# Two mixture-of-experts layers around a causal linear attention: every expert on every token, or tokens grouped by expert through DRAM

## What is computed

```python
def _L0_ffn_ref(h, router_w, rn_g, rn_b, w1, ln_g, ln_b, w2, on_g, on_b):
    h_norm = layer_norm(h, rn_g, rn_b)
    g = jax.nn.softmax(jnp.einsum('bsd,ed->bse', h_norm, router_w), axis=-1)
    top2_w, top2_idx = jax.lax.top_k(g, 2)
    top2_w = top2_w / (jnp.sum(top2_w, axis=-1, keepdims=True) + EPS_GATE)
    hid = jnp.einsum('bsd,edh->bseh', h, w1)               # 4 experts, 256 -> 512
    hid = jax.nn.relu(layer_norm(hid, ln_g, ln_b))
    expert_out = jnp.einsum('bseh,ehd->bsed', hid, w2)     # 512 -> 256
    ...
    out = jnp.sum(top2_out * top2_w[..., None], axis=-2)   # the two best experts
    return layer_norm(out, on_g, on_b)
x = x + 0.5 * _L0_ffn_ref(_layernorm(x), ...)
x = x + _L0_attn_ref(_layernorm(x), ...)   # 16 heads of 16: V K^T summed over the tokens so far, times Q
x = x + 0.5 * _L0_ffn_ref(_layernorm(x), ...)
```

## Time and profile before

| | us |
|---|---|
| median of 3 runs | 1239.57 |
| lowest and highest run | 1239.57, 1240.85 |
| span of the profiled execution | 1236.4 |
| preparation, to the first matmul of layer 1 | 63.3 |
| first mixture layer (63.3 to 513.2) | 449.9 |
| attention (513.2 to 809.5) | 296.3 |
| second mixture layer (809.5 to 1225.7) | 416.2 |
| behind its last matmul | 10.7 |

### The profile page before, as it was taken

One profiled execution on the slowest core, in us unless ns is written; L12 is line 12 of the kernel. 1 busy time (PEld: TensorE's weight loads), 2 busy tenths in 40 slices (PEclk: granted clock), 3 DMA queues, 4 the chain that ended last, 5 costly groups with the idle time before them and its releaser, 6 DMA issues.

```text
span 1236.4 us, 25066 instructions
## 1 busy us (share of the span) xinstructions
PE 1140.2 (92%) x8694; PEld 731.9 (59%) x8694; DVE 948.3 (77%) x2150; ACT 512.8 (41%) x878; POOL 672.0 (54%) x1039
## 2 busy tenths in 40 slices
PE   4669799999999999889999999889999999999996
PEld 4335456656566566656666666556566665666664
DVE  5678787887978878657777777578879787797875
ACT  4353324233342424456665666442333424334131
POOL 2365546454565544498778777543555654546360
PEclk9789989999999999999999999899999999999998
DMA  9002000000000000000000000000000000000000
GB/s 286 4 1 69 1 1 2 1 2 1 0 0 0 1 2 1 19 18 15 11 13 18 17 18 18 1 2 2 17 1 18 1 19 18 0 17 1 19 18 17
DMA packets 29037, 20.69 MB, mean 17 GB/s; under 512 B 7812, under 2 KB 27784, under 8 KB 28808
## 3 DMA queue, kind: packets, MB, share of 16 engines
q1 hardware_dynamic: 24112, 18.36, 5.4%
q10 hardware_dynamic: 4824, 1.07, 0.5%
HBM read 11.03 MB, written 4.19 MB: 12 GB/s over the span
## 4 chain that ended last, share of the span: by engine, by line
PE 48%; DVE 19%; issue 16%; POOL 10%; ACT 4%; DMA 2%; DVEq 1%; ACTq 0%; POOLq 0%
PE bank L1547 7%; PE bank L1549 6%; PE bank L1548 6%; DVE area L674 5%; DVE area L682 4%; PE bank L1532 4%; PE bank L1534 4%; PE bank L1533 4%; DVE area L655 4%; PE bank L1506 4%; POOL area L487 3%; PE bank L1555 2%; PE bank L1557 2%; PE bank L1556 2%; DMA betas<-in_L_ffn_ln_b_dram 2%
## 5 line engine op out<-in xcount | busy, mean ns | idle before, releaser
L1256 ACT ACTIVATE area<-area 128x512 f16<-128x512 f32 x256 | 160.9, 630 | 387.9 <-DVE area L674 386.1
L1547 PE MATMUL bank<-w2h,area 128*128 128x256 f16 x1024 | 281.3, 275 | 12.9 <-DVE area L693 7.2
L1548 PE MATMUL bank<-w2l,area 128*128 128x256 f16 x1024 | 280.5, 274 | 0.0
L1549 PE MATMUL bank<-w2h,area 128*128 128x256 f16 x1024 | 280.5, 274 | 0.0
L674 DVE SCALAR_TENSOR_TENSOR area<-area,betas,bank 128x512 f32<-128x512 f32 x256 | 189.9, 743 | 46.0 <-PE bank L1534 37.6
L682 DVE SCALAR_TENSOR_TENSOR area<-area 128x512 f16<-128x512 f32 x256 | 188.7, 737 | 20.3 <-ACT area L1256 17.1
L1532 PE MATMUL bank<-hTh,w1h 128*128 128x512 f16 x512 | 195.5, 382 | 6.7 <-DVE area L674 6.7
L1533 PE MATMUL bank<-hTl,w1h 128*128 128x512 f16 x512 | 195.1, 381 | 0.0
L1534 PE MATMUL bank<-hTh,w1l 128*128 128x512 f16 x512 | 194.9, 381 | 0.0
L696 DVE SCALAR_TENSOR_TENSOR area<-bank,coef,area 128x256 f32<-128x256 f32 x192 | 92.1, 482 | 79.3 <-PE bank L1549 78.1
L487 POOL TENSOR_TENSOR area<-area 128x512 f16<-128x512 f32 x96 | 119.9, 1274 | 45.1 <-ACT area L1300 44.9
(11 more groups left out here) (233 smaller groups left out, 2109.6 us busy)
## 6 DMA issues: line engine op xcount, KB each, us to landing
X<-in_L_attn_x_dram SPq DMA_DIRECT2D x8, 512.0 KB, 7.1
area<-area SPq DMA_DIRECT2D x128, 32.0 KB, 2.0
out_dram<-X SPq DMA_DIRECT2D x7, 512.0 KB, 2.9
area<-in_L_ffn_w_dram SPq DMA_DIRECT2D x4, 512.0 KB, 9.9
X<-in_L_ffn_w_dram SPq DMA_DIRECT2D x2, 1024.0 KB, 15.7
area<-in_L_ffn_ln_g_dram ACTq DMA_DIRECT2D x1, 1024.0 KB, 6.1
out_dram<-X SPq DMA_DIRECT2D x4, 128.0 KB, 1.7
area<-in_L_attn_Wq_dram SPq DMA_DIRECT2D x1, 256.0 KB, 9.2
```

Source lines behind the costliest of these rows:

```text
L1256: act.activation(Rh[:, e % 2, m, :], V[:, a % NV], ACT.Relu).then_inc(s_Rh, 1)
L1547: pe.matmul(dst, Rh[:, e % 2, k, rows], w2h[:, e, k, :], start=(k == 0), stop=False)
L1548: pe.matmul(dst, Rh[:, e % 2, k, rows], w2l[:, e, k, :], start=False, stop=False)
L1549: last = pe.matmul(dst, Rl[:, e % 2, k, rows], w2h[:, e, k, :], start=False, stop=(k == HC - 1))
```

## The change

A mixture layer no longer runs every expert on every block. Its 32 tiles are two groups of 16. For each group:

- **Routing** goes by quads of four tiles. Row statistics (bn_stats and bn_aggr) are on DVE, the powers on POOL, the normalised rows on ACT as float16 high parts with DVE's low parts (`hrow`), the transposes, logits and a prefix sum of the choices (a triangular matrix) on PE, the softmax on ACT and DVE. DVE then gives each token and chosen expert a place in that expert's region (`place`), and at the end of a group tables: for each of 35 slot tiles of 128 places its expert (`etab`) and first row in DRAM (`rtab`), and for each token where its two results will lie (`pos`).
- **Scatter.** POOL writes each tile's rows (high and low part, 1 KB a token) to DRAM by indirect DMAs, one for the first and one for the second choice of the tile's tokens, 32 in a group, and four with rows of zeros behind the last token of each expert.
- **Slot tiles**, 35 in a group and 70 in a layer, run in 35 pairs. For each, SP reads its row number from the table into a register, loads the 128 rows plainly (`hs`, two pairs deep) and once more by a transposing DMA (`hT`, three pairs deep). PE reads the expert's number into a register and addresses all its weights by it: w1, w2 and the Gram matrices are now an array for each chunk, indexed by expert. The variance is computed for one expert, its root on POOL (`pair_std`), and PE transposes its two float16 parts to a row which DVE writes into partition 0 of `hT` (`std_rows`). Beta is row 0 of the chunk of w1 that meets it: one input row of w1 was subtracted from all others beforehand, as normalised rows have a zero sum. Layer 1 has thereby beta in its product; `hidden`, V, `sdB` and `sel` are gone, and ACT and DVE take the relu's parts from the bank. Layer 1 has 128 columns, layer 2 256 as before.
- **Results.** ACT scales a slot tile's result to SBUF (`scale_out`) and SP stores it to DRAM. For each token tile POOL gathers the first and the second expert's rows by two indirect DMAs, two tiles deep; ACT multiplies the first by its gate, DVE adds the second, normalises and adds to X. In the last layer SP stores each tile of X.

The next group is routed inside the pairs 0 to 13 of the layer (row statistics from pair 0, scatters in pairs 4 to 11, pads in 12), and the first group's tokens are gathered in pairs 19 to 28. The second group's 16 token tiles follow behind the last pair. The second layer's first group is routed ahead of its first pair. Attention is as before but stands alone: its weights' preparation and its first block do not lie in a mixture block, and no block of the second layer is prepared in its last chunks. All hardware loops are written out. The maxima over partitions in the preparation (POOL before) are transposes and small matmuls on PE.

```diff
+            def load_slots(S):                                   # SP
+                G, J = group(S)
+                if J == 0:
+                    for k in range(GQ):
+                        sp.wait_ge(sc_h[k], 32 * TB * (G + 1))
+                    sp.wait_ge(sc_p[G % 2], 16 * E * (G // 2 + 1))
+                    sp.wait_ge(r_tab, G + 1)
+                r, k = S // 2 % R_HS, S % 2
+                wait(sp, b_h2, S // 2 - R_HS + 1)
+                row = sp.value_load(rtab[0:1, G % 2, J:J + 1], min_val=0, max_val=(E - 1) * REG + (GT - 1) * P)
+                sp.dma_start(hs[:, r, k].rearrange("p c d -> p (c d)"),
+                             slots_in[G % 2][bass.ds(row, P), :]).then_inc(l_hs[S % (2 * R_HS)], 16)
+                wait(sp, b_A, 2 * (S // 2 - R_HT + 1))
+                sp.dma_start_transpose(hT[:, S // 2 % R_HT, k], slots_in[G % 2][bass.ds(row, P), :]
+                                       ).then_inc(l_hT[S % (2 * R_HT)], 16)
...
+                for k in range(2):                               # POOL, scatter(Q, j)
+                    pool.indirect_dma_start(slots_in[G % 2],
+                                            bass.IndirectOffsetOnAxis(spos[:, Q % 2, k, j:j + 1], 0),
+                                            hrow[:, t].rearrange("p c d -> p (c d)"), None
+                                            ).then_inc(sc_h[Q % GQ], 16)
...
+            def gather(i):                                       # POOL
...
+                wait(pool, c_acc, i - R_C + 1)
+                for k, d in enumerate((yA, yB)):
+                    pool.indirect_dma_start(d[:, i % R_C], None, slots_out[G % 2],
+                                            bass.IndirectOffsetOnAxis(pos[:, G % 2, k, t:t + 1], 0)
+                                            ).then_inc(g_y[i % R_C], 16)
...
+            def expert(S):                                       # PE
...
+                return pe.value_load(etab[0:1, G % 2, J:J + 1], min_val=0, max_val=E - 1)
...
             def layer1(...):
-                cols = slice(m * P, (m + 1) * P)
-                o = bank[m][:, :]
-                for c in range(KC):
-                    pe.matmul(o, w1h[:, e, c, cols], hTh[:, par, c, :], start=(c == 0), stop=False)
-                    pe.matmul(o, w1h[:, e, c, cols], hTl[:, par, c, :], start=False, stop=False)
-                    last = pe.matmul(o, w1l[:, e, c, cols], hTh[:, par, c, :], start=False, stop=(c == KC - 1))
+                a = hT[:, p % R_HT, S % 2]
+                for m in range(HC):
+                    o = bank[S % 2][:, m * P:(m + 1) * P]
+                    for c in range(KC):
+                        pe.matmul(o, w1h[c][m][:, bass.ds(e, 1), :], a[:, c], start=(c == 0), stop=False)
+                        pe.matmul(o, w1h[c][m][:, bass.ds(e, 1), :], a[:, KC + c], start=False, stop=False)
+                        last = pe.matmul(o, w1l[c][m][:, bass.ds(e, 1), :], a[:, c], start=False, stop=(c == KC - 1))
...
+                for p in range(NP):                              # PE, mixture(f)
+                    S = 2 * (p0 + p)
+                    if 1 <= p <= GP:
+                        rows_T(u1 + p - 1)
...
+                    if p + 1 < NP:
+                        nxt = [expert(S + 2), expert(S + 3)]
+                        grams(p0 + p + 1, nxt)
+                    layer1(S, e[0])
+                    if p >= 1:
+                        layer2(S - 1, last)
+                    layer1(S + 1, e[1])
+                    if 1 <= p <= GP:
+                        router(u1 + p - 1)
+                    if p + 1 < NP:
+                        std_T(p0 + p + 1)
+                    layer2(S, e[0])
+                    last, e = e[1], nxt
+                layer2(S + 1, last)
```

2165 lines of the change are left out of this document (1125 added, 1040 removed).

## The result

| | us, median | to the kernel before, with 95% interval |
|---|---|---|
| before | 1239.57 | |
| changed | 1433.46 (1426.42 to 1434.17) | 1.155 (1.152 to 1.158) |

A forecast was written before the change was run, and what follows sets the result against it. The prediction took the mixture layers to be bound by the PE array, DVE next. 70 pairs at 11.0 us, 770, plus 640 outside the pairs gave a span of 1410 and a time of about 1415 us, range 1190 to 1680.

The forecast's parts named there:

- The array's need is 357 us less: Mixture layers' matmuls on PE: 140 slot tiles at 3.08 us, 431 us, in place of 788.
- Light pairs at 10.5 us: PE's cost of two slot tiles with nothing beside them: matmuls, register steps, expert loads, transposes; 6.8 to 15.9.
- Pairs with tokens at 11: Nine later pairs of a layer, with two tokens summed and normalised on DVE beside them: 11 us each.
- The ring: Dependency through DVE, PE and ACT from one pair to the next: 11.7 us with a choose, 9.9 without.
- First matmul of layer 1 at 112: Preparation and first routing: 63 us before the change, together 112 after it.
- 64 us behind each layer: 16 tokens gathered, weighted and normalised with nothing beside them, POOL and DVE alternating at 3.5 us each.
- The second routing 75: Second layer's first group routed with nothing beside it: 18 us to positions, 36 scatters at 1.2, 12 to fill.
- All seams: 640 forecast: Everything outside the pairs: preparation 112, tokens behind layers 128, attention 320, second routing 75, last stores 5.
- The signs: What the changed kernel's profile should show if the forecast holds, such as PE well under 70% busy in mixture layers.
- A: Rival, chance 0.20: register steps and loads hide behind the array; pairs 8.6 to 9.9 us, span 1242 to 1333.
- C: Rival, chance 0.17: faster than before, PE remaining array-bound with less array time; 1107 to 1237 us.
- B: Rival, chance 0.19: dearer register steps, loads, register-addressed matmuls or transposing DMA; 13 to 15.5 us a pair, 1550 to 1725.

The follow-up runs named there:

- fixed_expert: Changed kernel with PE taking weights at fixed addresses, no expert number loaded (wrong experts): 1359.4 us.
- the other series: Later side-by-side measurement in which the unaltered changed kernel took 1399.8 us, where the first gave 1433.5.
- std_early: Changed kernel with DVE doing the next pair's std parts right behind its variances, ahead of token and routing steps: 1351.1 us.
- gather_deep: Changed kernel with buffers for gathered tokens four tiles deep and not two: 1423.3 us.
- plain_scatter: Changed kernel with plain DMAs to fixed rows from POOL for the indirect scatters and pads (results wrong): 1377.5 us.
- plain_T_again: Changed kernel with plain DMAs of the same bytes for the transposing ones (results wrong), repeated beside the unaltered changed kernel: 1398.8 us.
- changed_again: The changed kernel itself, unaltered, measured again in a later series: 1399.8 us.
- loads_only: Changed kernel with expert numbers loaded and checked but unused, all weights at fixed addresses (wrong experts): 1330.2 us.
- both: Changed kernel with std parts early on DVE and fixed experts without loads together (wrong experts): 1231.1 us, 0.994 of the kernel before.
- one_load: Changed kernel with one expert number loaded per mixture layer and used for all its slot tiles (wrong experts): 1357.9 us.

## Why the prediction was right, point by point

Slower was given 0.81, and 1433 is 18 us above the 1415 of the forecast. The range, 1190 to 1680 us, holds the kernel before too, so that the time lies in it says little; the terms say more.

- **The array's need is 357 us less.** Borne out by the pace that it rests on. In fixed_expert a light pair lasts 6.6 us where 6.16 were worked out for the array from the earlier trace rows; 0.3 of the rest are the transposes of the std parts.
- **Light pairs at 10.5 us** (6.8 to 15.9; the least values of its terms add up to 7.0). 8.7 measured. By the light pair that ends at 319.31, term by term: layer 1 takes 3.7 for 3.8, layer 2 2.7 for 2.6 (the gap at the head left out), the variance matmuls 1.05 for 0.9, the transposes and waits 0.3 for 0.8, and the loads of the two expert numbers cost 0.9 for 2.4. The loads are the term that was mis-sized. Each was put at 1.0 us from a bound in the earlier trace rows; the profile has 298 ns in the median, 1.2 us for the two with their checks, and about half of that ran while the array still had work. By the Trainium skill's 0.6 us, which the prediction gives beside its own sum, the term would be 1.6, nearer but still too long.
- **Pairs with routing at 11.5.** 11.5 (10.8 in the other series).
- **Pairs with tokens at 11.** 13.6. The ring was seen and added up to 9.9 without a choose, but with DVE's token work beside it and not in it. The order of DVE's program puts two sums, and with them ACT's weighting and the gathers, ahead of the std parts. std_early takes exactly that out.
- **70 pairs at 770 us.** 749.7. Light pairs forecast 1.8 us too long and token pairs 2.6 too short nearly cancel, which is luck.
- **First matmul of layer 1 at 112.** 146. DVE's routing of the four quads took until 111, 20 us longer than the 91 of the sum; some 11 scatters at 1.27 and four pads follow until 129, and then 17 us to layer 1 where 12 were put. These 34 us are the largest error of one item of the sum, and what makes DVE's part 20 us longer was not taken apart.
- **64 us behind each layer.** 61.7 and 63.6. 1.2 for a gather was close to the 1.27 measured. The wait of a gather for the sum two tiles earlier, which was pointed out ahead of the prediction, held nothing up (gather_deep); POOL and DVE alternate because POOL's power waits for DVE.
- **Attention 320.** 308.0: the first projection 48 us in (42 forecast), the chunks at 8.37 and not at the 8.98 of the earlier trace rows.
- **The second routing 75.** 94.1 (86.6 in the other series); plain_scatter puts 22 of the 86.6 to POOL's indirect issue beyond that of plain DMAs.
- **All seams: 640 forecast, 681.3 measured**, pairs 770 forecast, 749.7 measured: the span is 21 us off, and that it is no more is luck again, since one part is 41 us too low and the other 20 too high. In the other series, with a span of 1398.2, the sum would be 12 us too high.
- **The signs.** Of those named, the pairs' 370 to 400 us (373.9 and 375.8), the two stretches behind the layers and units well above 0.165 us came; PE busy "well under 70%" did not in the pairs (80%, and 69% with the tokens behind them), nor did 112 us to the first matmul of layer 1. None of the signs of being wrong came: the waits of L1616 for the slots' rows (28.3 and 31.6 us) are the two fills of the pipeline, and with plain DMAs (plain_T_again) they are only 1.6 and 1.8 us shorter than in changed_again.
- **The rivals.** A (register steps and loads hidden) did not come true: neither is hidden in the changed kernel, though the loads would be without the steps (loads_only). both gives 1231 with neither steps nor the wait on DVE, so C, a faster kernel, needed both edits and not one: its mark was 8.5 us a pair, and in that run they take 8.0 in the mean. B's slow transposing DMA is excluded by plain_T_again, 1 us, and its slower issue of matmuls through a register by one_load.

So where did the array's 357 us go? 116.4 of them came through: the pairs take 749.7 us where the blocks took 866.1. The rest stayed in the pairs, as 2.1 us of register steps, and of the loads that they uncover, in each light one (70 us in all, loads_only) and as the ring over DVE, ACT and POOL in the others (std_early: 72 to 82 us). Even with both out, in both, the 70 pairs take some 560 us (70 times 8.03) for 431 of array work; which engine holds them then was looked at for the token pairs alone. Against the 116.4 stand 82.7 of longer preparation, 94.1 of the second routing and 125.3 of tokens behind the layers, 302.1 in all, in which there is little or nothing for PE, and 11.7 of attention less 2.8 at the end: 302.1 + 11.7 - 2.8 - 116.4 = 194.6.
